# Wide cross attention takes its shifts off on VectorE, and the projections' norm moves from ScalarE to VectorE

## The reference

```python
x = x + _L0_xattn_ref(ctx_1024, _layernorm(x), ...)   # 8 heads of width 64
# keys and values: the 1024 context rows and the 512 rows of x, 1536 in all
# out = softmax(q k^T / sqrt(64)) v, then Wout
```

```python
x = x + part @ Wout;  next_in = (x - mean) / sqrt(var + 1e-5)
```

## Time and profile before

| what | us |
|---|---|
| median of three runs | 2459.78 |
| the profiled execution, its own time | 2452.8 |
| its span from the first to the last instruction | 2450.9 |
| wide cross attention, from the first row product to the end of the last scaling | 327.8 to 626.5 |
| of these: five units of the same length, counted from copy to copy | 384.10 to 558.17 |
| the ten projection and norm stages | 15 to 21 each |

### The profile page before, as it was taken

One profiled execution on the slowest core, in us unless ns is written; L12 is line 12 of the kernel. 1 busy time (PEld: TensorE's weight loads), 2 busy tenths in 40 slices (PEclk: granted clock), 3 DMA queues, 4 the chain that ended last, 5 costly groups with the idle time before them and its releaser, 6 DMA issues. The chain is left out here.

```text
span 2450.9 us, 32488 instructions
## 1 busy us (share of the span) xinstructions
PE 1874.7 (76%) x11486; PEld 930.0 (38%) x11509; DVE 1449.7 (59%) x2587; ACT 1090.1 (44%) x1814; POOL 837.9 (34%) x759
## 2 busy tenths in 40 slices
PE   5786979999775677676756787999758468899844
PEld 3344422222443444445643553333236335222223
DVE  3544244442475999994235447999534463787476
ACT  2343123444443444542322342888723244366646
POOL 1000024444143999993121032666631303000012
PEclk9898989999896988986877899999979789699967
DMA  5610461110019014003225517221133102633000
GB/s 162 168 28 30 167 209 61 49 42 14 18 39 230 18 21 83 1 2 120 91 63 143 164 49 203 63 57 38 47 139 106 44 18 97 159 76 65 10 1 18
DMA packets 172242, 190.65 MB, mean 78 GB/s; under 512 B 14708, under 2 KB 138686, under 8 KB 171046
## 3 DMA queue, kind: packets, MB, share of 16 engines
q1 hardware_dynamic: 169012, 180.20, 26.8%
q0 software_dynamic: 3072, 8.39, 1.1%
HBM read 124.17 MB, written 68.30 MB: 79 GB/s over the span
## 5 line engine op out<-in xcount | busy, mean ns | idle before, releaser
L3003 POOL TENSOR_TENSOR a2x_masked<-a2x_masked,tall_rows 128x512 f32<-128x512 f32 x128 | 163.2, 1276 | 111.6 <-ACT a2x_masked L2965 111.6
L1333 ACT ACTIVATE experts<-a1x_scores 128x1024 f32<-128x1024 f32 x128 | 124.0, 1021 | 155.4 <-PE a1x_scores L1264 155.4
L828 DVE TENSOR_REDUCE ctx_then_heads<-a0x_rows 128x2 f32<-128x1024 f32 x88 | 107.8, 1225 | 131.9 <-PE a0x_rows L670 131.9
L3014 DVE TENSOR_REDUCE a3x_row_most<-a3x_ring 128x1 f32<-128x512 f32 x256 | 159.2, 682 | 39.1 <-PE a3x_ring L2861 39.1
L652 POOL TENSOR_TENSOR a0x_pair_sums<-a0x_probs_T 128x1024 f32<-128x1024 f32 x48 | 112.9, 2352 | 164.2 <-ACT a0x_probs_T L774 164.2
L3014 DVE TENSOR_REDUCE a2x_row_most<-a2x_ring 128x1 f32<-128x512 f32 x256 | 162.4, 679 | 3.7 <-DMA a0a_qs<-a0a_shift 1.9
L1370 POOL TENSOR_TENSOR a1x_tree<-experts 128x1024 f32<-128x1024 f32 x64 | 150.3, 2349 | 35.4 <-ACT experts L1333 35.3
L1302 DVE TENSOR_TENSOR experts<-experts,a1x_inverse_total 128x2048 f32<-128x2048 f32 x64 | 145.7, 2276 | 4.4 <-ACT a1x_inverse_total L1346 4.4
L2958 ACT ACTIVATE a3x_probs_T<-a3x_scores_T 128x1024 f32<-128x1024 f32 x128 | 123.2, 1018 | 47.1 <-PE a3x_scores_T L2888 47.0
L1253 PE MATMUL a1x_scores<-a1x_qs,a1x_ks 96*128 96x128 bf16 x1024 | 92.5, 244 | 63.5 <-ACT experts L1333 44.7
L2958 ACT ACTIVATE wide_rows<-a2x_masked 128x1024 f32<-128x1024 f32 x128 | 135.9, 1062 | 1.4 <-POOL a2x_masked L3003 1.4
(11 more groups left out here) (672 smaller groups left out, 4244.1 us busy)
## 6 DMA issues: line engine op xcount, KB each, us to landing
v_scr<-p0x_vout SPq DMA_DIRECT2D x24, 256.0 KB, 2.0
k_scr<-p0x_x SPq DMA_DIRECT2D x24, 256.0 KB, 2.3
ctx_then_heads<-k_scr SPq DMA_DIRECT2D x8, 768.0 KB, 4.9
a0x_vs<-v_scr SPq DMA_DIRECT2D x8, 768.0 KB
experts<-in_L_ffn_w SPq DMA_DIRECT2D x8, 768.0 KB, 6.6
v_scr<-experts SPq DMA_DIRECT2D x16, 256.0 KB, 2.2
a1x_vs<-v_scr SPq DMA_DIRECT2D x16, 256.0 KB, 5.7
v_scr<-p2x_vout SPq DMA_DIRECT2D x16, 256.0 KB, 2.8
```

What stands on the lines that cost most here:

```text
L828: nc.vector.tensor_reduce(rm[:, qt, :, c], row_psum(r)[:, :, :], AX.X, ALU.max).then_inc(row_most, 1)
L1333: nc.scalar.activation(ex[:, n % E, 8 * half:8 * half + 8, :], sp_[:, g % 3, :, :, :].rearrange("p i j q -> p (i j) q"), ACT.Exp).then_inc ...
L3003: nc.gpsimd.tensor_tensor(sm[:, i % 2, 1, :], sm[:, i % 2, 1, :], full[1][:, i // 2 % KT, :], ALU.add).then_inc(pool_masked, 1)
L3014: nc.vector.tensor_reduce(rm[:, u % 2, h * QT + qt:h * QT + qt + 1, part], ring[:, row_place(r) % 3, 0:n], AX.X, ALU.max).then_inc(row_mos ...
```

## The change

In the wide attention the second, bf16 product of every step is gone. The unit's shifts are brought into all partitions once: VectorE first reduces the maxima to `most8` (128x8) and then copies each of the 8 numbers 128 times into `mz` (128x1024 bf16, by reading one element again and again). TensorE transposes this with eight products in place of four, so that PSUM holds the shift of each query in every partition, and ScalarE copies 128x1024 float32 to `shifts`. At every step VectorE subtracts `shifts` from the scores in PSUM (`take_off`) and writes `sm` in SBUF (three buffers), and `exp` reads that. `score(n + 1)` now waits for the subtraction n - 1 instead of the exponential.

In the norm stages VectorE normalizes (subtract the mean, multiply by 1/std) and the bias is gone; its order is add, inverse of the tile before, statistics, normalize the tile before, aggregate. Where the source isn't transposed yet, two tiles are transposed and copied ahead instead of one.

```diff
@@ wide_attention_stage, TensorE
                     for qt in range(QT):
-                        mm = nc.tensor.matmul(rp[:, 0, qt * P:(qt + 1) * P], mz[:, qt, :], core.ident_bf[:, :],
-                                              start=True, stop=True)
+                        for h in range(HG):
+                            mm = nc.tensor.matmul(rp[:, h, qt * P:(qt + 1) * P], mz[:, qt, h, :], core.ident_bf[:, :],
+                                                  start=True, stop=True)
@@ score(n)
-                        pe.wait_ge(most_moved, u + 1)
                         qk_ready(pe, u)
                     if n >= 2:
-                        pe.wait_ge(expd, n - 1)
+                        pe.wait_ge(less, n - 1)
...
-                        mm = nc.tensor.matmul(sT[:, n % 2, h, :], minus[hs, :], mT[hs, u % 2, :], start=False, stop=True,
-                                              skip_group_check=True)
@@ ScalarE
-                    nc.scalar.activation(pT[:, n % R, :, :], sT[:, n % 2, :, :], ACT.Exp).then_inc(expd, 1)
+                    nc.scalar.activation(pT[:, n % R, :, :], sm[:, n % 3, :, :], ACT.Exp).then_inc(expd, 1)
...
-                    nc.scalar.copy(mT[:, u % 2, :], rp[:, 0, :]).then_inc(most_moved, 1)
+                    nc.scalar.copy(shifts[:, u % 2, :, :], rp[:, :, :]).then_inc(most_moved, 1)
@@ VectorE
-                    nc.vector.tensor_reduce(mz[:, :, 0::hd], rm[:, :, :, :], AX.X, ALU.max).then_inc(most, 1)
+                    nc.vector.tensor_reduce(most8[:, :, :], rm[:, :, :, :], AX.X, ALU.max).then_inc(rounded, 1)
+                    dve.wait_ge(rounded, u + 1)
+                    if u:
+                        dve.wait_ge(most_turned, u)
+                    nc.vector.tensor_copy(mz[:, :, :, :], most8[:, :, :].unsqueeze(3).to_broadcast([P, QT, HG, P])
+                                          ).then_inc(most, 1)
+                def take_off(n):
...
+                    if n >= 3:
+                        dve.wait_ge(expd, n - 2)
+                    nc.vector.tensor_tensor(sm[:, n % 3, :, :], sT[:, n % 2, :, :], shifts[:, u % 2, :, :], ALU.subtract
+                                            ).then_inc(less, 1)
...
+                take_off(0)
+                for n in range(N):
+                    if n + 1 < N:
+                        take_off(n + 1)
+                    for r in range(rows_done(n - 1), rows_done(n)):
+                        row_maximum(r)
@@ out_norm_stage, ScalarE
-                    if 1 <= s <= NT:
-                        normalize(s - 1)
@@ VectorE
-                    nc.vector.tensor_scalar(bias[:, t:t + 1], mv[:, t, 0:1], rstd[:, t:t + 1], -1.0, ALU.mult, ALU.mult
-                                            ).then_inc(minus_mean, 1)
+                    nc.vector.tensor_scalar(normed[:, t, :], dst[:, t, :], mv[:, t, 0:1], rstd[:, t:t + 1],
+                                            ALU.subtract, ALU.mult).then_inc(xn_done, 1)
```

More of the change, by code:

```diff
@@ L575, in wide_attention_stage @@
         v_in = [st.sem(f"v_in{i}") for i in range(2)]
-        minus_in, zeroed, cast, rowed, row_most, most, most_turned, most_moved = (
-            st.sem(x) for x in ("minus", "zeroed", "cast", "rowed", "row_most", "most", "most_turned", "most_moved"))
+        cast, rowed, row_most, rounded, most, most_turned, most_moved, less = (
+            st.sem(x) for x in ("cast", "rowed", "row_most", "rounded", "most", "most_turned", "most_moved", "less"))
         scored, expd, valued, counted = (st.sem(x) for x in ("scored", "expd", "valued", "counted"))
@@ L769, in exp @@
                 def exp(n):
-                    act.wait_ge(scored, n + 1)
+                    act.wait_ge(less, n + 1)
                     if n >= R:
@@ L778, in turned_most @@
                     if u >= 2:
[L779 to L780 removed]
+                        act.wait_ge(less, KT * (u - 1))
+                    nc.scalar.copy(shifts[:, u % 2, :, :], rp[:, :, :]).then_inc(most_moved, 1)
                 def u_out(u):
@@ L823, in _, with row_maximum @@
             def _(dve):
-                def row_maximum(u, i):
+                def row_maximum(r):
+                    u, i = divmod(r, NR)
                     qt, c = rows[i]
-                    r = NR * u + i
                     dve.wait_ge(rowed, r + 1)
+                    if i == 0 and u:
+                        dve.wait_ge(rounded, u)
                     nc.vector.tensor_reduce(rm[:, qt, :, c], row_psum(r)[:, :, :], AX.X, ALU.max
                                             ).then_inc(row_most, 1)
+                    if i == 8 and u >= 2:
+                        scale(u - 2)
+                    if i == NR - 1:
+                        maximum(u)
                 def maximum(u):
[L832 to L837, removed]
                     dve.wait_ge(row_most, NR * (u + 1))
-                    dve.wait_ge(zeroed, 1)
+                    if u:
+                        dve.wait_ge(most, u)
+                    nc.vector.tensor_reduce(most8[:, :, :], rm[:, :, :, :], AX.X, ALU.max).then_inc(rounded, 1)
+                    dve.wait_ge(rounded, u + 1)
                     if u:
                         dve.wait_ge(most_turned, u)
-                    nc.vector.tensor_reduce(mz[:, :, 0::hd], rm[:, :, :, :], AX.X, ALU.max).then_inc(most, 1)
+                    nc.vector.tensor_copy(mz[:, :, :, :], most8[:, :, :].unsqueeze(3).to_broadcast([P, QT, HG, P])
+                                          ).then_inc(most, 1)
+                def take_off(n):
+                    u, kt = divmod(n, KT)
+                    dve.wait_ge(scored, n + 1)
+                    if kt == 0:
+                        dve.wait_ge(most_moved, u + 1)
+                    if n >= 3:
+                        dve.wait_ge(expd, n - 2)
+                    nc.vector.tensor_tensor(sm[:, n % 3, :, :], sT[:, n % 2, :, :], shifts[:, u % 2, :, :], ALU.subtract
+                                            ).then_inc(less, 1)
                 def scale(u):
@@ L848, in scale @@
                                             ).then_inc(ao_done, 1)
[L850 to L853, removed]
+                for r in range(NR):
+                    row_maximum(r)
+                core.landed(dve)
+                take_off(0)
[3 more added lines that the diff above has]
+                    for r in range(rows_done(n - 1), rows_done(n)):
+                        row_maximum(r)
                 scale(U - 2)
@@ L995, in add, with statistics @@
                     nc.vector.tensor_tensor(dst[:, t, :], dst[:, t, :], term, ALU.add).then_inc(added, 1)
+                def statistics(t):
                     dve.wait_ge(added, t + 1)
```

63 lines of the change are left out of this document (33 added, 30 removed).

## The result

The changed kernel takes 2479.58 us (median of 4 runs, 2474.39 to 2485.53), the kernel before 2459.41 us on the same chip. The ratio is 1.0084, with a 95% interval of 1.0054 to 1.0113: slower by 0.8%, where 2455 was predicted with a range of 2441 to 2465. Timed once more, the ratio was 1.0064 (1.0050 to 1.0077). The profiled execution took 2474.39 us.

The account below looks back on a forecast made before the run. TensorE was taken to bound the wide attention, and no engine is full in the norm stages. Attention +17 and norm -22 gave -5: 2452.8 becomes 2447.8, or 2455 on the median's scale, range 2441 to 2465.

Parts of the forecast that it names:

- the hand-overs: Wide attention: waits of TensorE for other engines, 1.4, 0.6, 0.2 and 0.2 us a unit besides the copy's length.
- Unit of the wide attention, 34.8 + C: Wide attention: a unit keeps its 34.8 us, the removed product's gain being spent, and the maxima copy's length comes on top.
- C: Wide attention: length of VectorE's copy of the maxima, taken as 2.6 us, with bounds 0.68 and 3.15.
- The lock that rows 8 suggested: Wide attention: VectorE's copy stands still until GpSimd's pair addition ends, then takes 0.55 us more.
- the 1.4 for late rows: Wide attention, steps without `count`: row products wait for VectorE's row maximum, up to 0.26 us each, 1.4 a unit.
- The terms 0.6: Wide attention: `spread_den` waits for the last row maximum too, 0.6 us more a unit.
- 0.2 behind the turning: Wide attention, after the maxima are transposed: TensorE waits 0.2 us a unit for ScalarE's copy.
- TensorE's own work falls to 32.4: Wide attention: removing the second product, less four more small products, takes TensorE's work from 34.8 to 32.4 us a unit.
- a rival with a chance of 0.03: Wide attention: TensorE's clock falls to 0.9 because it waits, costing 28 us, total 2483; chance 0.03.
- Attention in sum: Whole wide attention: seven copies of 2.6 us, less 3.0 at the end, plus 2 at the start, +17 us.
- Norm, -22: All ten norm stages: shorter tile periods and earlier stage ends give -22 us, bounds -17 and -25.
- The round trip of 1.27: Norm stages: the chain between VectorE and ScalarE sets a tile's period, 1.27 us, used as 1.30.

Follow-up runs that it names:

- the filled wait: Changed kernel plus twelve zero-stationary bf16 products of 512 columns per unit between counting and turning of the maxima: 2469.54 us, ratio 1.0036 to the kernel before.

## Why the prediction was wrong

The wide attention by itself was to cost 17 us and costs 30.8 (298.7 to 329.5), and the norm stages gave back 19.4 instead of 22. That is 16 of the 25 us between 2455 and 2479.6; the others stay open (last point). In a unit, 39.43 against 37.4, the clock makes 1.25 (39.43 - 38.18), the hand-overs 0.64 and the copy 0.14.

- **Unit of the wide attention, 34.8 + C.** The C in it was right. The copy queues: C was taken as 2.6 and is 2.70, and it goes into the unit one to one (2.74). The lock that rows 8 suggested is shown by one added wait, which takes the copy to 0.69. The Trainium skill says the same (SBUF — State Buffer, SBUF: two separate sides): whoever starts first holds the ports to its end. The copy of 1024 elements in 0.69 us, as fast as the one-source instruction of rows 6 (0.676), also agrees with the Trainium skill's statement that one element read again and again by a one-source instruction runs in the two-port mode (Vector Engine (DVE) Microarchitecture Reference, 5.1 Performance modes), the one that no row before could show.
- **The hand-overs** (1.4 + 0.6 + 0.2 + 0.2) were mis-sized by 0.64 a unit: without the copy a unit is 35.44, not 34.8. The mis-sized term is the 1.4 for late rows. Without the copy they are 2.03 late in a unit: 0.35 to 0.43 in four steps and 0.12 to 0.22 in three, where the prediction had at most 0.26 in a step. The terms 0.6 (`spread_den`, 0.57 measured) and 0.2 behind the turning (0.21) were right. Without the copy the wide attention takes 303.2, +4.5 where the terms without C give 17 - 18.2 = -1. The five equal units make 3.1 of the difference. The rest lies at its ends, where traces of unchanged kernels differ by 1.9 too.
- **The step that failed** is "TensorE's own work falls to 32.4", priced at a clock of 1.00 throughout. The wait ahead of the turning (2.81 us in each of these units, 2.83 predicted) lets the clock fall in four of five units, and work behind it runs at 1.2 GHz: 463.3 - 455.5 = 7.8 us. The prediction had this as a rival with a chance of 0.03, and argued it away by a stretch whose mean busy share was 85%. TensorE's longest single wait in that stretch is 1.05 us, so it could not speak for one of 2.8. This step alone doesn't make the miss: 2479.6 less 7.8 is still above the range, and the late rows and the open part below are in it too. The rival's price, 28 us for a uniform 0.9, was wrong as well. That its 2483 lies near the measured time is chance.
- **Attention in sum**: +17 predicted; for the wide attention by itself +30.8 measured = 4.5 (no copy) + 18.7 (copy, 321.8 - 303.2) + 7.7 (clock, 329.5 - 321.8).
- **Norm, -22.** Measured -19.4. The round trip of 1.27, used as 1.30, is 1.25. The four self-turning stages do not reach it in their first two gaps (2.31 and 1.72 in o2a), since TensorE starts them at its lower level. The time to the first square root rose by 0.38 (o2x: 3.76 to 4.14), where 0.22 was taken. So these four stages give 12.6 us where the terms had 17.3, and the six others give 6.8 where they had 5.4. The two-ahead turning, which the prediction counted on for hiding TensorE, is needed for it: 4.1 us.
- **What stays open.** Attention and norm give +10.3. The medians differ by 20.2 us in the first timing and by 17.5 in the second. The two halves timed apart give 1.0042, about +10.3. The remaining 7 to 10 us can't be placed. In the traces the untouched stages take 1829 to 1847 us, and 1833 and 1844 for one and the same kernel, so I can't tell a cause from chance.

## What to carry to other kernels

When a change makes TensorE wait in one piece, look at the granted clock of the stretch behind the wait and not at the mean busy share. Here 2.81 us of idle time cost up to another 2.3 us a unit, while 0.8 us cost nothing more. The VectorE copy within SBUF that started 0.21 us behind a GpSimd addition cost what was left of the addition and 0.55 us more: 2.70 instead of 0.69. Before you put such a copy on the path, let GpSimd wait for it, or have TensorE read the column repeatedly. Where TensorE must wait, products that change nothing can keep its clock up: twelve of them did so here in every unit.

## What the runs showed of the hardware that I had not expected

TensorE's clock fell after idle times of 2.81 us in some units and not in others of the same execution: it stayed at 1.00 in 388.51:426.63, with the same wait of 2.81. In the units with turnings at 456.73 and 576.16 it fell about 1 us after the wait, with TensorE at work again. What decides this is not shown here. The Trainium skill tells of a gate that throttles by default and that activity releases (TensorE: Matmul & The Clock Gate, Part 1), which agrees with the filled wait (clock 1.00 in all five units). A stationary operand that reads one column 128 times works, and its eight products take 0.61 us, as with a copied tile in the filled wait.
